# Moving a head's output copy ahead of the GELU burst and a row scaling one tick later in a two-block attention kernel

## What is computed

```python
# block 0: attention of x over ctx, only batch 0 of its result is used
att  = softmax((x @ Wq.T) (ctx @ Wk.T)^T / sqrt(32)) (ctx @ Wv.T)
x    = x + att[0]
# block 1, for each of the 8 sequences
q    = layer_norm(x, gq, bq) @ Wq
k, v = split(layer_norm(ctx, gkv, bkv) @ Wkv)
x    = x + softmax(q k^T / sqrt(32)) v @ Wproj + bproj
h    = gelu(layer_norm(x, gm, bm) @ W1 + b1)      # exact GELU, hidden width 2048
x    = x + h @ W2 + b2
```

## Time and profile before

| | |
|---|---|
| time, median of 3 runs | 1836.07 us (1834.27 to 1836.93) |
| span of the profiled execution | 1833.4 us |
| TensorE busy | 1730.2 us, 94% of the span |
| ScalarE busy | 1156.9 us, 63% |
| VectorE busy | 1082.3 us, 59% |
| GpSimd busy | 933.7 us, 51% |
| mean granted TensorE clock | 0.982 of full |

### The profile page before, as it was taken

The page is one execution under the profiler, slowest core; times in us unless marked ns, Lnnn a source line. Parts: engine busy times, 40 slices in busy tenths (PEclk is TensorE's granted clock), DMA queues, the critical chain, the costliest instruction groups (busy, mean ns, idle before and its releaser), DMA issues.

```text
span 1833.4 us, 23939 instructions
## 1 busy us (share of the span) xinstructions
PE 1730.2 (94%) x7488; PEld 1328.0 (72%) x7488; DVE 1082.3 (59%) x1860; ACT 1156.9 (63%) x1935; POOL 933.7 (51%) x778
## 2 busy tenths in 40 slices
PE   6899998987899899999999999999999999999898
PEld 5677776765666677777777767777777777777686
DVE  4566664576776566666666665666666666564322
ACT  3677774587877675766766676667667665774231
POOL 0355531287874465466555554655556445555331
PEclk8999999999999999999999999999999999999999
DMA  6688954897645664576577556756755765567262
GB/s 233 217 295 276 301 210 153 266 319 248 209 130 166 169 196 117 167 227 181 153 216 199 139 155 188 200 130 194 231 156 159 200 189 146 162 198 243 94 215 92
DMA packets 157102, 354.69 MB, mean 193 GB/s; under 512 B 29232, under 2 KB 47792, under 8 KB 156080
## 3 DMA queue, kind: packets, MB, share of 16 engines
q1 hardware_dynamic: 101744, 174.63, 32.3%
q10 hardware_dynamic: 55232, 178.53, 30.3%
HBM read 251.51 MB, written 82.08 MB: 182 GB/s over the span
## 4 chain that ended last, share of the span: by engine, by line
PE 65%; ACT 10%; DVE 7%; POOL 6%; DMA 5%; issue 5%; SPq 1%; ACTq 1%; DVEq 1%; POOLq 0%
PE ps_d L862 43%; PE ps_o L883 11%; PE ps_t L916 5%; PE ps_s L901 5%; DMA q_st<-negmax_t 3%; DVE negmax L1175 1%; POOL p_lo L1285 1%; ACT p_hi L1015 1%; ACT ps_d L936 1%; POOL stage L1306 1%; ACT ps_t L1022 1%; ACT ht L991 1%; DVE stats L1132 1%; PE ps_d L792 1%; ACT h_st L1006 1%
## 5 line engine op out<-in xcount | busy, mean ns | idle before, releaser
L1285 POOL TENSOR_TENSOR p_lo<-p_full,p_hi 128x512 fp32r<-128x512 f32 x288 | 371.3, 1289 | 592.0 <-ACT p_full L1022 590.6
L1015 ACT ACTIVATE p_hi<-ps_t 128x512 fp32r<-128x512 f32 x576 | 344.8, 599 | 380.2 <-PE ps_t L916 379.5
L1175 DVE TENSOR_REDUCE negmax<-ps_s 128x1 fp32r<-128x512 f32 x576 | 389.8, 680 | 146.3 <-PE ps_s L901 145.9
L862 PE MATMUL ps_d<-hT,w_r 128*128 128x512 f32 x1536 | 421.1, 395 | 3.6 <-DVE hT L1080 1.4
L862 PE MATMUL ps_d<-w_r,g_s 128*128 128x512 f32 x1536 | 392.2, 395 | 5.6 <-DMA w_r<-w_scratch 5.6
L862 PEld LDWEIGHTS ps_d<-hT,w_r 128*128 128x128 f32 x1536 | 290.1, 189 | 75.9 <-DVE hT L1080 2.9
L862 PEld LDWEIGHTS ps_d<-w_r,g_s 128*128 128x128 f32 x1536 | 292.1, 190 | 72.1 <-issue 7.8
L1188 DVE TENSOR_TENSOR p_lo<-ps_t,p_hi 128x512 fp32r<-128x512 f32 x288 | 198.5, 689 | 235.2 <-ACT ps_t L1022 233.8
L883 PE MATMUL ps_o<-p_hi,v_s 128*65 128x512 f32 x576 | 234.7, 407 | 37.0 <-ACT o_raw L1029 27.3
L916 PE MATMUL ps_t<-q_st,k_st 97*128 97x512 f32 x576 | 233.2, 405 | 12.1 <-DMA q_st<-negmax_t 11.8
L901 PE MATMUL ps_s<-k_st,q_st 96*128 96x512 f32 x576 | 233.2, 405 | 6.7 <-DVE negmax L1175 6.6
(11 more groups left out here) (99 smaller groups left out, 2166.4 us busy)
## 6 DMA issues: line engine op xcount, KB each, us to landing
w_r<-w_scratch ACTq DMA_DIRECT2D x214, 512.0 KB, 5.0
w_r<-w_scratch SPq DMA_DIRECT2D x42, 512.0 KB, 4.7
v_scratch<-v_out SPq DMA_DIRECT2D x36, 520.0 KB, 3.5
k_scratch<-kq_out SPq DMA_DIRECT2D x36, 512.0 KB, 3.7
q_st<-q_scratch SPq DMA_DIRECT2D x144, 128.0 KB, 4.5
k_st<-k_scratch SPq DMA_DIRECT2D x144, 128.0 KB, 4.3
o_ab<-o_raw SPq DMA_DIRECT2D x144, 128.0 KB, 3.7
v_s<-v_scratch ACTq DMA_DIRECT2D x31, 520.0 KB, 6.2
```

The lines of the kernel that those rows point to most:

```text
L862: ins = nc.tensor.matmul(bank(u), lhs[a], rhs[b], start=(i == 0 and m == 0), stop=(i == 3 and m == 2))
L1015: act.activation(p_hi[:, c], ps_t[:, c % 2], ACT.Exp, scale=SCALE)
L1175: dve.tensor_reduce(negmax[:, h % 2, c:c + 1], ps_s[:, c % 2], AX.X, ALU.max, negate=True).then_inc(s_maxed, 1)
L1285: pool.tensor_tensor(p_lo[:, c], p_full[:, (by_gpsimd(s) - 1) % 2], p_hi[:, c].bitcast(F32), ALU.subtract).then_inc(p_pool_split, 1)
```

## The change

In a tick that has both a GELU burst and a head's end, ScalarE now issues the copy `o_raw<-ps_o` ahead of the burst instead of behind the exponentials. In all other ticks the copy stays where it is. And the row scaling of the MLP normalisation is issued one tick later for sequences 1 to 7: in tick 175 instead of 174, and in the burst's own ticks 239, 303, 367, 431, 495, 559, behind their exponentials, instead of the tick before. Sequence 8 keeps its place.

```diff
     at = tuple(emptied("out", i, t) for t in range(TC))
-    return at, at[-1], (at[-1] + 1,) * 4
+    return at, at[-1], (at[-1] + (1 if i == NP - 1 else 2),) * 4
...
+        def move_head(h):
+            act.wait_ge(pv_done, h * TC + TC)
+            if h >= 2:
+                act.wait_ge(o_placed[(h - 2) % G], ((h - 2) // G + 1) * (16 * PLACE_DMAS))
+            act.activation(o_raw[0:VW, h % 2], ps_o[0:VW], ACT.Identity).then_inc(o_moved, 1)
+
...
             for u in EVACUATED.get((tick, False), []):
                 evacuate(*u)
+            weighted = PLAN.pv_at.get(tick)
+            head_ends = weighted is not None and weighted % TC == TC - 1
+            if head_ends and tick in PLAN.bursts:
+                move_head(weighted // TC)
             for n, group in PLAN.bursts.get(tick, []):
...
-            s = PLAN.pv_at.get(tick)
-            if s is not None and s % TC == TC - 1:
-                h = s // TC
-                act.wait_ge(pv_done, s + 1)
-                if h >= 2:
-                    act.wait_ge(o_placed[(h - 2) % G], ((h - 2) // G + 1) * (16 * PLACE_DMAS))
-                act.activation(o_raw[0:VW, h % 2], ps_o[0:VW], ACT.Identity).then_inc(o_moved, 1)
+            if head_ends and tick not in PLAN.bursts:
+                move_head(weighted // TC)
             for u in EVACUATED.get((tick, True), []):
                 evacuate(*u)
```

## The result

| | before | after |
|---|---|---|
| time, median | 1837.18 us (20 executions) | 1843.2 us (20 executions) |
| ratio to before | | 1.0027 (95%: 1.0016 to 1.0038) |
| span of the profiled execution | 1833.4 us | 1843.0 us |
| mean granted TensorE clock | 0.982 | 0.982 |

What follows compares the result with a forecast made beforehand. TensorE, busy 94% of the span, was taken to bound the kernel, losing time only where it waits. Terms 14.7 - 1.8 - 1.1 + 1.2 - 2.5 = +10.5 us on the 1836.07 us median gave 1846.6 us, range 1839 to 1855.

Steps and rivals of the forecast that it cites:

- ScalarE, ticks 302 to 310: At tick 303's burst and five like it, ScalarE's next exponentials come 0.4 us later; by ScalarE alone each gains some 0.2 us.
- GpSimd, ticks 304 to 310: The moved b2 addition delays two `p_lo`, so TensorE waits in ticks 308 and 310: +2.7 us in each of six stretches.
- The row DMA: TensorE's 0.25 us wait on a row DMA at 923.40 is absorbed; over six stretches, 6 x (2.7 - 0.25) = +14.7 us.
- The six bursts 255, 319 and so on: At tick 319 and its five like, the copy fits into ScalarE's idle time before the GELU's table load: 0.3 each, -1.8 us.
- Tick 195: The 5.56 us copy wait goes, but tick 197's score matmul still waits for VectorE's chunk: -1.1 us, not -5.56.
- Sequence 1: Ticks 174 to 180: scaling behind tick 175's copy delays the addition and tick 178's `p_lo`: +1.2 us, bounds -1.8 and +2.5.
- The clock: Falls of TensorE's clock in three of six stretches cost 5.1 us; half taken as gained, -2.5, ends -5.1 and +5.1.
- all copy waits go: Rival: every TensorE wait on the copy at the bursts disappears, -20 us, 1816 us; chance 0.02.
- GpSimd's queue takes the addition in: Rival: the addition delays the second `p_lo` by under 1.06 us plus TensorE's lead; -9 us, 1827 us; chance 0.06.
- Only the first `p_lo` is late: Rival: +1.7 instead of +2.7 us per stretch and all clock falls go; +1.9 us, 1838 us; chance 0.07.
- The clock falls in every stretch: Rival: TensorE's clock falls in all six stretches, clock term +5.1; +18 us in all, 1854 us; chance 0.15.

## Why the prediction was right, and where its size was off

Step by step, in the order of the prediction:

- **ScalarE, ticks 302 to 310: right.** Counted from tick 302's score matmul (888.74 before, 890.68 after) the table load was to start at 4.66 us and did at 4.63, the scalings were to end at 13.1 and did at 13.09. The copy fell into the gap in front of the GELU (its input's wait is now 1.07 us, and stands behind the copy). The next exponentials came 0.3 us later, forecast 0.4. What ScalarE leaves of the 2.16 us is shown by the kernel with the addition out of the way: its stretches take 44.7 us for the 45.1 of before, so 0.4 us stays, where the step had 0.2.
- **GpSimd, ticks 304 to 310: right, and it is the term that decided.** Counted in the same way the addition was to end at 21.4 us and did at 21.2; the two `p_lo` were to be ready at 23.9 and 29.0 and were at 23.9 and 28.8. TensorE's waits are 2.5 and 1.25 us. At full clock the first ten ticks of a stretch take 32.4 us for 29.8, 2.6 us more where the step had 2.7: **+15.7** for +16.2. The stretches of the kernel with only the addition moved are as long (47.5 us), and the one with it taken out of the way has none of it.
- **The row DMA: right that it is absorbed, and a little small.** The step took 0.25 us off each stretch, 1.5 in all, from the one wait that it had read. After, no stretch has any of it, and before they had **2.1** us of it together, most of it in three stretches.
- **The six bursts 255, 319 and so on: right**, -1.9 for -1.8.
- **Tick 195: -0.5 for -1.1, the step right.** The wait went to the transposed score matmul of tick 197 as the step says, which now waits 5.08 us. It starts 8.24 us behind the stretch's first score matmul in all six executions with the copy ahead and 9.36 in the five without, which is the 1.1. Behind it part of this is lost again: the clock falls in this stretch in all eleven executions, for longer or shorter, and ticks 195 to 202 take 20.1 to 21.3 us without the copy ahead and 19.8 to 20.8 with it, a mean of 20.6 and of 20.3.
- **Sequence 1: 0.0 for +1.2, and the step was wrong.** TensorE arrives at tick 180 as the step let it: its score matmul comes 16.2 us behind that of tick 174 in both kernels. But ScalarE is faster than the step had it. It needs 2.0 us, not 3.1, for tick 175's evacuation, exponentials and copy, and its scaling starts at 562.92, 5.2 us behind tick 174's score matmul, where the step had 6.8. So the addition and the `p_lo` of tick 178 follow sooner: that one is ready at 575.29 and is wanted at 575.78, where the step had it 1.2 us late. TensorE's wait of 2.99 us on the copy in tick 176 has become one of 2.21 us on `aT` in tick 178. With the scaling moved and the addition out of the way the stretch takes 40.2 to 40.7 us, with the addition behind it 40.4 and 40.8, so that the queue costs a few tenths there at most.
- **The clock: the term that was mis-sized most.** "I take half of the 5.1 as gained, -2.5". By the first ten ticks the three falls of before cost 4.7 us and the three of after 0.3: **-4.4 us**. The 5.1 itself was somewhat too large, since its windows from burst to burst hold the row DMA too, a part of which the step thus counted twice. What failed is the half. The step had the reason why a fall would cost nothing, "GpSimd sets the time up to 917.75", and said that a fall behind the first wait is hidden and one behind the second is not. In the profiled execution all three fell at the first wait (at 23.6 to 24.4 us of the stretch, the matmul starts at 24.0) and none behind the second, so that nearly all was gained, close to the step's good end of -5.1. Where the clock would fall the step could not know, so the size of this term is in part chance.

By terms: 15.7 for the queue, -2.1 for the row DMA, -1.9, -0.5, 0.0, -4.4 for the clock and the rest of -0.2 give +6.6 us, against 10.5 forecast. Of the 3.9 between them the clock makes 1.9, sequence 1 makes 1.2, and the others add up to 0.8. What the medians show, 5 to 6 us, is this sum to within what one profiled execution can say.

Of the rivals, "all copy waits go" and "GpSimd's queue takes the addition in" are refuted by ticks 308 and 310. "Only the first `p_lo` is late" is refuted by the 1.25 us. "The clock falls in every stretch" is refuted by three at full clock; and the three that fell cost 0.3 us together, far from the 5.1 that the rival put to six. The Trainium skill (TensorE: Matmul & The Clock Gate, HAM oscillation) has its rule on recurring waits from a kernel that waits 3 to 5 us for a DMA in every tile, longer than the recurring waits here, so that the prediction stretched it when it let all six stretches fall by it. The runs say this: in the eight executions with a wait of about 2 us or more in each stretch the clock fell in 1 to 5 stretches of six, 26 of 48 in all, which agrees with the rule only in part; in the three executions where the addition is late and the scaling behind the burst, and no wait of a stretch but two on a row DMA (0.52 and 0.84 us) is over half a microsecond, it fell in none of 18. That waits and falls go together here is shown; that each wait brings a fall is refuted for waits of this length.

## What to carry to other kernels

Before an instruction is moved in an order written by hand, list what is derived from its place: here the scaling took a 4.6 us addition with it, out of an idle gap of another engine and in front of two results that TensorE wanted, and that was all of the loss. A wait that has one name may have a second behind it: taking the copy's wait away alone only moved 2.16 us on to the next matmul that needed the same engine's work, and it took the later scaling and the addition out of the way together, here with the copy ahead as well, to gain 0.6%, or 0.9% with the roundings moved too. And a fall of the clock is worth its time only where TensorE sets the time, 1.5 to 1.6 us in the kernel before; where another engine's queue does, it cost 0.0 to 0.15.

## What the runs showed of the hardware

A copy on VectorE (128x512, one operand) that starts beside a running GpSimd instruction ends 0.28 to 0.37 us after that instruction's end, in 253 of 255 cases in ten executions. In the other two it was passed over: it stood 4.85 us across four and 6.40 us across five instructions, where its shortest time is 0.42, and ended 0.29 us after the last one, when GpSimd had a gap. As a maximum of two operands it ends 0.54 to 0.59 us after the running instruction, in 29 of 30 cases, and GpSimd's next pair takes 2.96 us instead of 2.70. The Trainium skill (SBUF — State Buffer, Who interferes with whom) says that a copy may take the port pair that VectorE shares with GpSimd, and that who issues first holds it for the whole instruction. With the 253 copies, which wait for one instruction, the traces agree. By that rule the two long ones would also have lost one instruction of some 1.25 us at most; they lost four and five. Why it happened in one stretch of six, the same in both executions, while the copy took at most 1.5 us in the others, was not tried and stays open.
